# Two expert routings re-ordered: prefix scans, a start after twelve row moves, and a first expert loop that transposes four tiles ahead

## What is computed

```python
gates = softmax(x @ gate_w)                      # 2048 tokens, 8 experts
top_v, top_i = top_k(gates, 2); top_v /= sum(top_v)
h = gelu(x @ fc_w[e])                            # first block: 128 -> 512
out = sum_k top_v[k] * (h @ proj_w[e_k])
# fourth block: silu(x @ w_gate[e]) * (x @ w_up[e]), then w_down[e]
```

## Time and profile before

| what | value |
|---|---|
| runs, median | 620.51 us |
| the profiled execution | 617.3 us |
| its span, first to last instruction | 615.6 us |
| mean granted TensorE clock | 0.926 |
| busy share PE / DVE / ACT / POOL | 87% / 67% / 39% / 44% |
| chain that ended last: PE / DVE / issue | 73% / 20% / 4% |
| first routing and loop, roughly | 66 to 185 us |
| second routing and loop, roughly | 457 to 604 us |

### The profile page before, as it was taken

One profiled execution on the slowest core, in us unless ns is written; L12 is line 12 of the kernel. 1 busy time (PEld: TensorE's weight loads), 2 busy tenths in 40 slices (PEclk: granted clock), 3 DMA queues, 4 the chain that ended last, 5 costly groups with the idle time before them and its releaser, 6 DMA issues.

```text
span 615.6 us, 12275 instructions
## 1 busy us (share of the span) xinstructions
PE 537.0 (87%) x3780; PEld 456.0 (74%) x3781; DVE 410.1 (67%) x1482; ACT 239.9 (39%) x551; POOL 272.4 (44%) x505
## 2 busy tenths in 40 slices
PE   4999866998899899999999798989974399999992
PEld 2678553987896599898977675757763199999992
DVE  8878846322357885456689869888887556555573
ACT  3455233543454434444423233455531043334330
POOL 4464373888758108900000010546436368774332
PEclk9999657999997899999989989999995599999996
DMA  9998011322253100000000720004001112221233
GB/s 304 380 311 266 10 52 37 84 73 69 70 163 107 58 1 1 2 1 1 1 1 2 219 56 2 0 2 138 1 2 39 48 50 71 60 61 52 77 109 120
DMA packets 48153, 47.66 MB, mean 77 GB/s; under 512 B 6470, under 2 KB 37603, under 8 KB 47942
## 3 DMA queue, kind: packets, MB, share of 16 engines
q1 hardware_dynamic: 43558, 37.68, 20.5%
q0 software_dynamic: 4544, 9.38, 4.5%
HBM read 27.53 MB, written 19.51 MB: 76 GB/s over the span
## 4 chain that ended last, share of the span: by engine, by line
PE 73%; DVE 20%; issue 4%; ACT 1%; DMA 1%; another core or an unknown queue 1%; DVEq 0%; POOLq 0%; POOL 0%; SPq 0%; ACTq 0%
PE bank L2391 17%; PE bank L2402 10%; PE bank L1987 8%; PE bank L2183 4%; PE bank L2228 4%; PE bank L2267 4%; PE bank L2256 2%; PE bank L1976 2%; PE bank L1977 2%; PE bank L1978 2%; PE bank L1868 2%; PE bank L2325 1%; PE bank L2379 1%; PE bank L2218 1%; DVE stats L1095 1%
## 5 line engine op out<-in xcount | busy, mean ns | idle before, releaser
L2391 PE MATMUL bank<-xT,wcur 128*128 128x128 f32 x936 | 118.6, 277 | 6.6 <-ACT xT L880 3.6
L2391 PEld LDWEIGHTS bank<-xT,wcur 128*128 128x128 f32 x936 | 110.6, 192 | 10.0 <-issue 5.5
L627 POOL TENSOR_SCALAR var_eps<-mv 128x4 f32<-128x4 f32 (+2 forms) x12 | 2.8, 236 | 183.3 <-DVEq L1813 95.8
L684 POOL DMA_INDIRECT yt<-Y,dest_i x62 | 61.3, 989 | 50.7 <-ACT Y L896 32.0
L668 POOL DMA_INDIRECT xw<-XW,slot_i x64 | 63.3, 989 | 43.3 <-ACT xT L880 10.9
L1445 DVE COPY wcur<-WA 128x512 f32 x78 | 36.3, 466 | 50.3 <-PE bank L2391 26.4
L964 ACT ACTIVATE hT<-bank,b_cols 128x512 f32<-128x512 f32 x64 | 44.0, 688 | 63.1 <-PE bank L1978 62.5
L1987 PE MATMUL bank<-WC,hT 128*128 128x128 f32 x512 | 64.1, 280 | 0.0
L1987 PEld LDWEIGHTS bank<-WC,hT 128*128 128x128 f32 x512 | 61.7, 195 | 1.4
L1583 DVE SCALAR_TENSOR_TENSOR X<-bank,G,X 128x128 f32<-128x128 f32 x128 | 36.0, 343 | 32.7 <-PE bank L1987 27.4
L1460 DVE TENSOR_TENSOR hT<-gb,bank 128x512 f32<-128x512 f32 x39 | 26.8, 688 | 41.7 <-ACT gb L885 39.5
(11 more groups left out here) (406 smaller groups left out, 1182.6 us busy)
## 6 DMA issues: line engine op xcount, KB each, us to landing
xw<-pad_rows SPq DMA_DIRECT2D x34, 260.0 KB, 4.4
xrow<-xw SPq DMA_DIRECT2D x78, 65.0 KB
WA<-in_fc_dram SPq DMA_DIRECT2D x16, 256.0 KB, 4.7
YT<-yt SPq DMA_DIRECT2D x16, 256.0 KB, 3.6
WA<-in_pj_dram SPq DMA_DIRECT2D x8, 256.0 KB, 5.2
WB<-in_fc_dram SPq DMA_DIRECT2D x8, 256.0 KB, 4.9
WB<-in_pj_dram SPq DMA_DIRECT2D x8, 256.0 KB, 6.3
X<-in_x_dram SPq DMA_DIRECT2D x2, 512.0 KB, 4.4
```

The lines of the kernel that those rows point to most:

```text
L684: pool.indirect_dma_start(out=yt_dram, out_offset=bass.IndirectOffsetOnAxis(ap=dest_i[:, t:t + 1], axis=0), in_=y_slot(layer, t), in_offse ...
L2391: ins = pe.matmul(dst, wcur[:, s4, at:at + P], xT[s4 % 2][:, :], start=True, stop=True)
```

## The change

- `choices` reads the logits where PE left them (no copy); both running sums become one scan instruction each (`tensor_tensor_scan`). `ranks` has five small matmuls instead of three: two subtract what the scan carried over from the expert before.
- The table gets a sixth kind of segment (tiles 0 to 5), so that slots that are full after six tiles come first. Moves go tile by tile, both choices together; SP loads slots 0 to 4 after twelve moves, and slot 5 waits for the other four.
- `table_out` goes ahead of the last step of `places`. PE no longer waits for moves; the unused matmuls go from 8 to 0 and from 26 to 14.
- Set-up: the row product and the two first `later_m` go ahead, `values(1)` is split in two halves around the logits, `later_keys` goes to the end; ACT's sixteen masked copies of the keys go right behind `later_context`; DVE's part goes into `experts`, behind the first weights.
- POOL: in the first block the second group's moves follow the first group's after one pause.
- First loop only: a tile is transposed four slots ahead instead of three, into four banks and four places instead of two and two.

```diff
+SOON = 6
+SOON_ONLY = -(-(SOON * P * TOPK - PARTIAL) // P)
-KINDS = 5
+KINDS = 6
...
-                sp.wait_ge(scattered[0], 16 * MOVES * (layer + 1))
+                sp.wait_ge(scattered[0], 16 * TOPK * SOON * (layer + 1))
                 for t in range(SLOTS):
+                    if t == SOON_ONLY:
+                        sp.wait_ge(scattered[1], 16 * TOPK * (GT - SOON) * (layer + 1))
...
                 for tile in range(GT):
-                    scatter(layer, 0, tile, 0)
-                for tile in range(GT):
-                    scatter(layer, 0, tile, 1)
-                    if tile == GT // 2 - 1:
-                        pool.sem_inc(most_moved, 1)
-                pool.wait_ge(scattered[0], 16 * MOVES * (layer + 1))
+                    for choice in range(TOPK):
+                        scatter(layer, 0 if tile < SOON else 1, tile, choice)
+                pool.wait_ge(scattered[0], 16 * TOPK * SOON * (layer + 1))
                 if layer == 0:
-                    pool.wait_ge(setup_mm, B + 4 + B - 1)
+                    pause()
...
-                link(dve.tensor_tensor(ahead_a[:, g, PAD + 1:, :], both[:, g, 1:, :], both[:, g, 0:GT - 1, :], ALU.add))
...
+                dve.tensor_tensor_scan(upto_tile[:, g, 2:], both[:, g, :], ones_f[:, 0:E * GT], 0.0,
+                                       ALU.add, ALU.mult).then_inc(both_ready, 1)
...
+                    if g and k:
+                        table_out(layer)
                     link(dve.tensor_reduce(slot_f[:, k, :], pick[:, :, :], AX.X, ALU.add))
...
-                link(dve.tensor_copy(cum_b[:, pad:], lens[:, :]))
-                src, dst = cum_b, cum_a
-                for step in (1, 2, 4, 8, 16, 32):
-                    link(dve.tensor_tensor(dst[:, pad:], src[:, pad:], src[:, pad - step:pad - step + SEGMENTS], ALU.add))
-                    src, dst = dst, src
-                cum = src[:, pad:]
-                link(dve.tensor_tensor(upto[:, :], cum, lens[:, :], ALU.subtract))
+                link(dve.tensor_tensor_scan(cum[:, 1:], lens[:, :], ones_f[:, 0:SEGMENTS], 0.0, ALU.add, ALU.mult))
+                upto, past = cum[:, 0:SEGMENTS], cum[:, 1:]
...
+                dve.wait_ge(experts_known, layer + 1)
                 dve.wait_ge(in_experts[layer], 16 * (len(ups) + 1) * E)
                 for t in range(RING):
                     weights(t)
+                if layer == 0:
+                    values(1)
                 shares(layer, 1)
                 destinations(0)
-                done_counts(layer, tile_counts[layer])
+                done_counts(layer)
+                if layer == 0:
+                    split_row()
...
             def router(layer, n, gate_w):
                 if layer == 0:
                     later_context()
+                    later_row()
                 ranks(layer, 0)
+                if layer == 0:
+                    pe.wait_ge(dl_ready, 1)
+                    values(1, wv3, range(GB))
                 transposes(n, range(GB, B))
                 logits(n, range(GT, TILES), gate_w)
                 if layer == 0:
-                    later_keys()
+                    later_m(0)
+                    later_m(1)
                 ranks(layer, 1)
                 if layer == 0:
-                    values(1, wv3)
-                    later_row()
+                    values(1, wv3, range(GB, B))
                 table(layer)
                 if layer == 0:
-                    later_m()
+                    later_m(2)
+                    later_m(3)
+                    later_keys()
...
-                pe.wait_ge(most_moved, layer + 1)
-                warm((8, 26)[layer], 2)
+                warm((0, WARM)[layer], 2)
                 if layer == 0:
                     pe.wait_ge(m_evac, 2 * B)
+                    pe.wait_ge(s1_evac, 8)
                     pe.wait_ge(setup_evac, B + 3)
...
+                if layer == 0:
+                    pe.wait_ge(routed, GROUPS)
+                    tr_x(3, 3, 0)
+                ahead = 3 if layer else RING
+                steps = SLOTS - ahead
...
-                        tr_x(t + u + 3, (u + 3) % RING, i + (u + 3) // RING)
+                        tr_x(t + u + ahead, (u + ahead) % RING, i + (u + ahead) // RING)
                         up_mm(t + u + 2, (u + 2) % RING)
                         dn_mm(t + u, u, e, first=first and u < 2)
```

More of the change, by code:

```diff
@@ L321, in build @@
         PT = PT.rearrange("p (i c t) -> p i c t", i=2, c=HC)
[L322 to L326, removed]
+        spans = YT[:, 0:2, :].rearrange("p t f -> p (t f)")
+        lens, below = (spans[:, i * SEGMENTS:(i + 1) * SEGMENTS] for i in range(2))
+        found = spans[:, 2 * SEGMENTS:4 * SEGMENTS].rearrange("p (i s) -> p i s", i=2)
+        upper = spans[:, 4 * SEGMENTS:4 * SEGMENTS + 2 * E].rearrange("p (i e) -> p i e", i=2)
+        f12 = spans[:, 4 * SEGMENTS + 2 * E:4 * SEGMENTS + 3 * E]
         PT1 = [hT[2][0:K, :, :], hT[3][0:K, :, :], Y[0:K, 0:BT, :], Y[0:K, BT:2 * BT, :]]
@@ L369, in build @@
             sem(n) for n in ("lg_mm", "both_ready", "rank_mm", "routed", "dl_ready", "ex_ready"))
[L370 removed]
+        scattered = [sem(f"scattered{i}") for i in range(4)]
         table_ready, table_mm = (sem(n) for n in ("table_ready", "table_mm"))
@@ L912, in experts @@
                         step(i, u)
-                if unrolled < YROUNDS:
-                    with act.Fori(unrolled, YROUNDS) as i:
+                if unrolled < rounds:
+                    with act.Fori(unrolled, rounds) as i:
                         for u in range(YRING):
                             step(i, u)
-                for u in range(STEPS % YRING):
-                    step(YROUNDS, u)
-                activate(SLOTS - 1, (SLOTS - 1) % RING)
-                for t in range(STEPS, SLOTS):
+                for u in range(steps % YRING):
+                    step(rounds, u)
+                for t in range(steps, SLOTS - 2):
+                    activate(t + 2, (t + 2) % RING)
+                    if t < SLOTS - 3:
+                        y_copy(t, t % YRING, t // YRING)
+                for t in range(SLOTS - 3, SLOTS):
                     y_copy(t, t % YRING, t // YRING)
@@ L1068, in _ @@
                 tokens(1, q, 4 + q)
+            for b in range(GB):
+                later_m(b)
+            router(1)
+            for b in range(GB, B):
+                later_m(b)
             later_keys()
-            router(1)
-            later_m()
             experts(0)
@@ L1172, in first_keys, with split_row @@
                 keys(0, 0)
-            def later_setup():
-                values(1)
+            def split_row():
                 dve.wait_ge(r_read, 1)
@@ L1375, in table @@
+                upto, past = cum[:, 0:SEGMENTS], cum[:, 1:]
+                rows = slice(0, SLOTS)
+                dve.tensor_tensor(value[:, 0, :], flat_ends[:, 0:SEGMENTS], upto, ALU.subtract)
+                link(dve.tensor_scalar(below[rows, :], past[rows, :], place_no[rows, :], None, ALU.is_gt))
                 dve.tensor_tensor(value[:, 0, :], value[:, 0, :], tile_home[:, :], ALU.add)
-                rows = slice(0, SLOTS)
-                link(dve.tensor_scalar(below[rows, :], cum[rows, :], place_no[rows, :], None, ALU.is_gt))
@@ L1877, in first_m, with values @@
                           start=True, stop=True).then_inc(setup_mm, 1)
-            def values(i, wv):
+            def values(i, wv, batches=range(B)):
                 pe.wait_ge(ctx4_ready, 1)
-                for b in range(B):
+                for b in batches:
                     dst = bank[3 - 3 * i][:, b * P:(b + 1) * P]
@@ L2427, in experts @@
                 round_of(0, RING, first=layer == 0)
-                with pe.Fori(1, ROUNDS) as i:
+                with pe.Fori(1, steps // RING) as i:
                     round_of(i, RING)
-                round_of(ROUNDS, STEPS % RING)
-                up_mm(SLOTS - 1, (SLOTS - 1) % RING)
-                for t in range(STEPS, SLOTS):
+                round_of(steps // RING, steps % RING)
+                for t in range(steps, SLOTS - 2):
+                    up_mm(t + 2, (t + 2) % RING)
+                    if t < SLOTS - 3:
+                        dn_mm(t, t % RING, id_of(t))
+                for t in range(SLOTS - 3, SLOTS):
                     dn_mm(t, t % RING, id_of(t), last=True)
```

190 lines of the change are left out of this document (94 added, 96 removed).

## The result

The changed kernel took 608.81 to 616.16 us, median 615.12, beside a median of 620.56 for the kernel before: ratio 0.9889, interval 0.9852 to 0.9926, so 4.6 to 9.2 us, about 5.4 by the medians. The forecast was 607.0, 13.5 us less than before, within 599 to 616. The time fell inside the range, but among the times of rival A (610.5 to 615.5) and not of the forecast (601 to 610). The profiled execution took 614.5 us with a span of 612.4, 3.2 us less than before.

The account below looks back on a forecast made before the run. PE, busy 87% of the span, was taken as the bound outside the two routings. Second routing -9.5 and first -4.2 gave -13.7 on 617.3, 603.6; with the runs' median 3.2 above, 607.0 us was forecast, range 599 to 616.

Parts of the forecast that it names:

- rival A: First routing: table's round trip over PE held until POOL's burst ends; -7.5 us in all, 613; chance 0.20.
- Second routing, table: Second routing: DVE's shortened steps make the table known at about 478.0 in place of 485.94, -7.9 us.
- the links: Second routing: five DVE links after the table's running sum lose holds, fewer POOL moves being behind them; -1.0 us.
- `table_out` ahead: Second routing: the last step of `places` no longer stands before `table_out`; -2.9 us, bounds -1 and -3.1.
- I take -9.5: Second routing: first transpose at 484 to 485.5, loads ending last and not PE; -9.5 us, bounds -11 and -6.
- first transpose at 97.5 in place of 104.72: -7.2: First routing: table known at 93, then PE's last set-up and SP's first rows by about 96; bounds -9 and -4.
- +2 for the start-up: First loop's start: DVE's moved set-up delays buffer reloads, and four ahead needs the fifth load sooner; +2 us (0 to +3).
- slots 9 and 17 wait no more than before: First loop: second group's moves and the puts behind them come 8 us earlier, as the loop does; no cost.
- No warm-up is lost that matters: First routing: the unused matmuls dropped there cost nothing in clock, since real matmuls stand in their place.
- The slow stretch: First loop: 11 tiles 2.71 us apart while POOL issues without rest, 9.1 us excess; four ahead takes -1 (0 to -5).
- Rival B: Both routings: no hold is left, and four ahead covers the slow tiles; -22 us, 598.5; chance 0.12.
- Rival C: Loops: without the rest, hand-overs come on POOL's beat, 4.6 us a tile in the second loop; 625; chance 0.09.

Follow-up runs that it names:

- set three: Four kernels on chip 8, both kernels with traces; the kernel before had a median of 600.74 us.
- `a_base`: The changed kernel with asserted bounds on SP's put-count loads, on chip 4: 612.26 us, ratio 0.9795 to the kernel before.
- `b_norest`: The kernel before, POOL going on with the second group's moves after one pause, without the wait that made it rest: 622.59 us, ratio 0.9973.
- `a_soon16b`: The changed kernel with SP's first load held until all 16 moves landed, in both blocks, on chip 8: 602.17 us, ratio 1.0019.
- `a_warm26`: The changed kernel with 26 unused matmuls ahead of the second loop in place of 14: 596.54 us, ratio 0.9927.
- sets two and three: Four kernels each, on chips 2 and 8; the kernel before had medians of 601.01 and 600.74 us.
- set one: Four kernels on chip 4, testing POOL's missing rest against the depth of four; the kernel before had a median of 624.39 us.
- `a_three`: The changed kernel with three tiles ahead in the first loop in place of four: 615.89 us, ratio 0.9852.
- T1: Theory tested in the first four follow-up runs: POOL issuing without a rest holds the other engines' hand-overs; depth is of no account.
- `a_base2`: The changed kernel with asserted bounds on SP's put-count loads, run again on chip 8: 592.31 us, ratio 0.9849 to the kernel before.
- `a_rest`: The changed kernel, POOL holding the second group's moves until ACT has copied all set-up, in place of one pause: 612.32 us, ratio 0.9794.
- `a_late`: The changed kernel with 40 unused matmuls ahead of the first loop, to start it later: 598.92 us, ratio 0.9970.

## Why the prediction came out at two and a half times the gain

**Second routing, table.** Forecast -7.9, of which -0.8 is the first group's share; so -7.1 from the second look, and measured -6.1 (14.97 us from it to the start of the last cast, after it 8.85). By terms: the copy was to give 0.26 a group and gave nothing, since the addition that builds `both` now takes 0.46 in place of 0.22 and the scan starts 3.48 us after the first look as the prefix steps did (3.49). Prefix to scan -0.57 (-0.5 forecast), running sum to scan -2.57 (-2.5), the links -0.59 (-1.0), `table_out` ahead -2.67 (-2.9), and the steps between the two scans +0.28, which were not priced here at all: nearly all of it is that DVE waits 0.47 us for the counts in place of 0.18, behind five small matmuls of PE in place of three. The sixth kind of segment costs next to nothing. The scans themselves take 0.29 and 0.26; 0.3 was taken.

**Second routing, start.** The 14 matmuls took 4.89 (4.4 forecast; the clock was at 0.50 for 3.5 us of them and not for 2.6), PE began 1.33 after the table, and the first load went from 17.17 to 12.29 us behind the first look, -4.9 (-5.9). The step "I take -9.5" measured -8.5 at the first transpose (23.60 to 15.08), where the matmuls ended last and not the loads, and then 1.3 was lost by the fifth tile: ACT took up at 491.86 what was transposed at 490.24 to 490.51. That leaves the -7.2 of the block.

**What most of that gain was.** In set three the table of the kernel before was known 11.04 us after the first look, not 14.97. The holds between DVE's links (0.96, 0.47 in the earlier trace rows) and around the broadcast, which I counted as savings of the scans and of `table_out`, aren't there. The changed kernel's table takes 8.84 in that set and took 8.85 on record, so on record it happened to meet no hold; in `a_base` it takes 11.37, beside 14.95 in `b_norest`. That the table's term came out near its forecast is partly luck: a kernel before with holds stood beside a changed one without. Free of holds in both, the change saves 2.2 us of the table, the loads come 5.4 us earlier (16.73 to 11.36), and the block is 5.1 shorter.

**Which part of the change bears it.** In set three the loads end last in the kernel before, but only just: its 26 unused matmuls keep PE to the first transpose at 475.24, and PE then waits 0.45 us for the rows of the second. In the changed kernel the unused matmuls end last. So the parts need each other. `a_soon16b` holds the loads back, and the gain is gone to the last microsecond, and 1.1 more, since the clock has fallen again when the rows come: the earlier table, the shorter warm-up and the order of set-up give nothing without the start on twelve moves. `a_warm26` keeps 26 matmuls, and 2.8 of the 5.1 are left (26.15 to 23.37, across sets two and three, in which the changed kernel's block is 21.03 and 21.04). The start on twelve moves alone was not run; by PE's waits for the rows in the kernel before (0.20 and 0.45 us) I estimate that it would give under 1 us.

**First routing: the step that failed.** It is "first transpose at 97.5 in place of 104.72: -7.2", bounds -9 and -4. It came at 109.44, 4.7 later than before, and behind POOL's first move 34.97 us in place of 30.99. The table was on time (91.2, forecast 93, bounds 90 and 97); ACT was the one that was held, to 108.48, and I had named its held copy (9.74 idle at 96.53) but priced it only for the table. It was the kind of hold that rival A named, with a worse end: the hold outlasted POOL's burst by 14 us (94.67 to 108.48), while POOL went on with the second group's moves. That the missing rest made it so long is not shown. It is the only run with holds in which POOL did not stand idle there (2.62 to 4.56 us in the four of set one), and the only one with so late a start (109.44; 98.84 to 106.47 in those four). In `a_three` ACT made one copy in POOL's rest (95.39) and the next at 98.29 and 102.02, when POOL had gone on (97.59). That fits T1, but no run put the rest into the held case and took it out again. The missing rest is not enough by itself: in set three POOL goes on at 95.45 without one, and nothing is held. In set three, without holds, the same step measures -4.75 (24.64 to 19.89 us behind the first move): there the copies of `later_keys`, put last, end at 94.09, and PE waits 0.99 for them and then 0.58 for the rows.

**First loop.** The steps "+2 for the start-up" and "slots 9 and 17 wait no more than before" can be read in set three. From the first tile to the seventh (slot 6) it takes 9.86 us in place of 9.07, +0.8. Two things show in it: slot 6 waits 1.21 us for its rows (104.31), and the granted clock, which was 1.00 from 97 on before, fell to 0.60 at 96 and 0.50 until 99, after PE had been busy for 0.30 to 0.67 of each microsecond from 93 to 96. "No warm-up is lost that matters" was thus not quite so. Then slot 9 waits: POOL's eighth paced move is at 106.62 in place of 108.60, its load at 109.50, the transpose at 111.66 after 1.44 us of waiting; before 114.40 after 0.20. So slot 9 came 2.7 us earlier and not 4.8, because the moves do not come as much earlier as the loop does (95.45 in place of 97.62). And four ahead transposes each tile 1.90 us earlier against the products, so the products came 0.8 earlier, and the end of the block, with some late tiles, not at all: 101.34 us before, 101.37 after. Forecast was -4.2; with no hold the first block gives 0.0, with holds +3.4 in the pair on record. In set three the two blocks together give 5.1, while the medians are 8.1 apart and the traced spans 6.4: some of the whole gain lies outside both blocks and is not explained. That the second group's moves would begin 8 us earlier was right on record (103.07 to 95.36), and 2.2 in set three, where the rest was only 2.64.

**The slow stretch.** On record it went, and the forecast had it stay (priced there at 9.1; 104.72 in the earlier trace rows is two transposes, so 16 tiles and not 15 came ahead of it, at 1.76). But it was paid for ahead: 15.90 and 4.69 us of PE's waiting. In set one, slow tiles are in every kernel with three or four ahead, with a rest or without, at another place each time; in sets two and three they are nowhere for more than a few tiles. Rival B's condition (no hold left) is met in set three, but not its gain of 22 us: it is 8 there (600.42 to 592.31), since the kernel before has no holds to lose either. Rival C did not happen: the second loop keeps 2.79 us a tile.

The rule of the Trainium skill that was weighed (*SBUF — State Buffer*, *Who interferes with whom*: PE and ACT never wait on anyone) is about access to SBUF. Read as a rule on hand-overs it agrees with sets two and three (PE waits 0.99 us for ACT at the first transpose of `a_base2`) and not with the record or set one (15.90). No run shows what makes the difference.

**What stays open.** Why hand-overs are held in one set and not in another, with the same instructions; the chips differed, but so may have other things. That the held copies start at two places of POOL's beat says that its issues have a part in it. `a_rest` says that a rest of 4.6 us does not keep the slow tiles away, and `a_late` that POOL's stream alone does not make them. What a missing rest does in the held case is open, since no kernel of set one lacked it in its trace, and so is what a later start does there, since `a_late` ran only where nothing is held. A kernel that takes the moves off POOL's queue was not tried.

The best of the twelve is the changed kernel itself, with or without the memsets behind the puts (592.31, 593.81 and 591.88), and a_rest (612.32) is no better than it (612.26).

## What to carry to other kernels

Before a sum is made from idle times, ask of each whether it is the program's or a held hand-over: here 3.9 of the 6.1 us that the table gained were holds, and the same kernel in another set didn't have them. When a loop is to start earlier, list every wait on its first ten steps with the queue that ends it; an earlier start that meets a fixed stream (POOL's moves at 1.52 us) is given back. And where the loads and PE are ready within a microsecond of each other, shorten both or gain next to nothing: the earlier table and the shorter warm-up were worth nothing without the start on twelve moves, and with the old warm-up 2.3 of the 5.1 us were gone.

## What was not expected of the hardware

One program took 601 us in two sets and 624 in another, on three chips. The two traces of the kernel before have spans of 615.6 and 596.7, 18.9 apart: 15.1 in the first block (116.40 and 101.34), 4.7 in the second (30.82 and 26.15), 0.9 the other way ahead of the first move; the stages between agree to 0.2 us. Such a difference can thus sit wholly in the stretches in which POOL issues indirect DMAs beside the other engines.
